# Turning the rows of two expert mixtures: DMA transposes on ScalarE's queue in place of TensorE transposes

## What is computed

```python
# layer 0: x_flat (2048, 256); wg, wu (8, 1024, 256); wd (8, 256, 1024)
hidden = silu(x_flat @ wge.T) * (x_flat @ wue.T)
acc = acc + we[:, None] * (hidden @ wde.T)             # over the 8 experts
# layer 1: W1 (8, 256, 2 * 512), W2 (8, 512, 256), at most 640 rows for an expert
h = einsum('ecd,edf->ecf', exp_batches, W1)
inp, gate = split(h, 2, axis=-1)
exp_out = einsum('eci,eid->ecd', gelu(inp) * gate, W2) # then added up by token with its gates
```

## Time and profile before

| | us |
|---|---|
| median of three runs | 885.04 |
| lowest and highest of them | 881.98, 886.37 |
| span of the profiled execution | 889.0 |
| first mixture's block loop in the profile, about | 289 to 607 |
| second mixture's block loop in the profile, about | 709 to 889 |
| TensorE busy in the span | 700.3 (79%) |
| VectorE busy in the span | 547.8 (62%) |
| ScalarE busy in the span | 403.1 (45%) |
| GpSimd busy in the span | 302.8 (34%) |

### The profile page before, as it was taken

One profiled execution on the slowest core, in us unless ns is written; L12 is line 12 of the kernel. 1 busy time (PEld: TensorE's weight loads), 2 busy tenths in 40 slices (PEclk: granted clock), 3 DMA queues, 4 the chain that ended last, 5 costly groups with the idle time before them and its releaser, 6 DMA issues.

```text
span 889.0 us, 19049 instructions
## 1 busy us (share of the span) xinstructions
PE 700.3 (79%) x6278; PEld 550.1 (62%) x6278; DVE 547.8 (62%) x1322; ACT 403.1 (45%) x720; POOL 302.8 (34%) x306
## 2 busy tenths in 40 slices
PE   5476796989564799999999899996862098898981
PEld 4232454555354688888897798895531087777771
DVE  7768576887836545647556656547696446566441
ACT  1135466576513434646545555442552044546331
POOL 7505301416337422222121131232167414334342
PEclk9689799989776799999999999997875599999996
DMA  4562300601524542536344643425022555464332
GB/s 140 118 141 51 59 2 24 180 24 49 153 81 151 185 129 36 165 51 171 78 126 98 170 112 101 107 39 179 25 101 95 174 170 131 115 147 114 63 55 40
DMA packets 68418, 92.24 MB, mean 104 GB/s; under 512 B 14442, under 2 KB 54435, under 8 KB 68348
## 3 DMA queue, kind: packets, MB, share of 16 engines
q1 hardware_dynamic: 41788, 63.37, 24.1%
q0 software_dynamic: 14592, 16.24, 10.6%
q10 hardware_dynamic: 11968, 11.72, 5.3%
HBM read 64.21 MB, written 29.87 MB: 106 GB/s over the span
## 4 chain that ended last, share of the span: by engine, by line
PE 48%; DVE 18%; issue 11%; ACT 9%; POOL 5%; DMA 5%; ACTq 2%; another core or an unknown queue 1%; DVEq 0%; POOLq 0%; SPq 0%
PE ps L685 45%; POOL rows L631 3%; DVE probs L1726 3%; DVE mx L1591 2%; DMA out_x<-keys,row_to 2%; DVE keys L1804 2%; DMA probs<-rows 2%; ACT probs L1189 1%; ACT probs L1271 1%; ACT expo L1186 1%; DVE keys L1783 1%; ACT probs L1267 1%; PE ps L933 1%; DVE stats L1383 1%; ACTq L1252 1%
## 5 line engine op out<-in xcount | busy, mean ns | idle before, releaser
L1804 DVE TENSOR_TENSOR keys<-probs,ps 128x512 f32<-128x512 f32 x122 | 82.8, 687 | 177.3 <-ACT probs L1267 86.3
L685 PE MATMUL ps<-keys,slot 128*128 128x256 f16 (+1 forms) x1440 | 146.5, 263 | 5.4 <-DVE keys L1783 2.7
L685 PE MATMUL ps<-keys,probs 128*128 128x256 f16 (+1 forms) x1488 | 139.5, 255 | 5.1 <-DVE probs L1405 3.7
L685 PEld LDWEIGHTS ps<-keys,slot 128*128 128x128 f16 x1440 | 127.8, 99 | 22.8 <-issue 5.4
L685 PEld LDWEIGHTS ps<-keys,probs 128*128 128x128 f16 x1488 | 124.2, 98 | 19.0 <-issue 7.2
L575 POOL DMA_INDIRECT attended<-keys,row_to x42 | 67.2, 1601 | 166.0 <-ACT keys L1280 142.2
L1267 ACT ACTIVATE probs<-ps 128x512 f32<-128x512 f32 x122 | 71.4, 598 | 65.9 <-PE ps L685 63.7
L1280 ACT ACTIVATE keys<-ps,carried 128x256 f32<-128x256 f32 x80 | 33.5, 470 | 117.9 <-POOLq L580 41.6
L1809 DVE TENSOR_TENSOR probs<-keys,probs 128x512 f16<-128x512 f32 x122 | 83.3, 688 | 3.6 <-ACT probs L1271 1.9
L1271 ACT CAST probs<-keys 128x512 f16<-128x512 f32 x122 | 74.8, 614 | 22.0 <-DVE keys L1804 21.9
L1726 DVE TENSOR_TENSOR probs<-expo,probs 128x512 f16<-128x512 f32 x80 | 61.1, 775 | 34.1 <-ACT probs L1189 28.2
(11 more groups left out here) (285 smaller groups left out, 1145.7 us busy)
## 6 DMA issues: line engine op xcount, KB each, us to landing
inbox<-in_W SPq DMA_DIRECT2D x24, 512.0 KB, 3.9
probs<-rows ACTq DMA_DIRECT2D x44, 260.0 KB
inbox<-in_wg SPq DMA_DIRECT2D x16, 512.0 KB, 5.2
inbox<-in_wu SPq DMA_DIRECT2D x16, 512.0 KB, 3.7
inbox<-in_wd SPq DMA_DIRECT2D x16, 512.0 KB, 4.2
rows<-zeros SPq DMA_DIRECT2D x16, 260.0 KB
x<-in_x SPq DMA_DIRECT2D x4, 512.0 KB, 6.1
q_out<-queries SPq DMA_DIRECT2D x8, 256.0 KB, 2.1
```

The costliest lines, as they stand in the source:

```text
L685: return pe.matmul(o, l, r, start=start, stop=stop, **kw)
L1804: dve.tensor_tensor(h32[:, j % 2, :], s_act[:, j % 2, :], ps[:, 2 * (j % 2) + 1, :], ALU.mult).then_inc(S(r + "_h32"), 1)
```

## The change

TensorE's 8 transposes for each block go away, and so does VectorE's copy out of PSUM. In their place ScalarE issues two DMA transposes for each block, from `x_raw` to a new buffer `turned_raw` in SBUF, each of 128 rows by 512 float16 values, and VectorE copies `turned_raw` to `xbT`. Rows are loaded and turned one block further ahead: in block g ScalarE turns block g+2 (after its last cast and after `xbT` of block g+1 has been copied) and, behind the scaling of `yb`, loads block g+3. The load waits until the turned rows of block g+2 have landed and their gates have been read, since there is still one `x_raw`. VectorE reads the gates for block g+2 instead of g+1. Ahead of the loop ScalarE loads and turns blocks 0 and 1 and loads block 2. Below, the pieces stand in the order TensorE, ScalarE, VectorE.

```diff
-AHEAD = MAXBLK + 2
+AHEAD = MAXBLK + 3
...
+        turned_raw = sb("turned_raw", [P, 2 * KC, BLK], F16)
...
-                def turn_block(g):
-                    pe.wait_ge(S(r + "_xraw"), g * 16 + 16)
-                    for hf in range(2):
-                        for part in range(4):
-                            last = pe.transpose(psh[:, 6, part * BLK + hf * P:part * BLK + (hf + 1) * P],
-                                                x_raw[:, hf, part * P:(part + 1) * P], identh[:, :])
-                    last.then_inc(S(r + "_xbT_ps"), 1)
...
-                    turn_block(g + 1)
                     pe.wait_ge(S(r + "_y"), g + 1)
...
+                def turn(g):
+                    wait_counted(act, S(r + "_xraw"), g * 16 + 16)
+                    for hf in range(2):
+                        act.dma_start_transpose(turned_raw[:, :, hf * P:(hf + 1) * P], x_raw[:, hf, 0:2 * D]).then_inc(S(r + "_turned"), 16)
+
+                def load_behind(g):
+                    wait_counted(act, S(r + "_turned"), g * 32)
+                    wait_counted(act, S(r + "_carried"), g)
+                    load(g)
...
-                    act.wait_ge(S(r + "_xbT_ps"), g + 3)
-                    act.wait_ge(S(r + "_carried"), g + 2)
-                    load(g + 2)
+                    wait_counted(act, S(r + "_xbT"), g + 2)
+                    turn(g + 2)
                     split(pairs)
                     act.wait_ge(S(r + "_down"), g + 2)
                     wait_counted(act, S(r + "_added"), g + 1)
...
                     ins.then_inc(S(r + "_y"), 1)
+                    load_behind(g + 3)
...
                 load(0)
+                turn(0)
                 act.wait_ge(S(r + "_padded"), 16 * (E - 1))
-                act.wait_ge(S(r + "_xbT_ps"), 2)
-                act.wait_ge(S(r + "_carried"), 1)
-                load(1)
+                load_behind(1)
+                act.wait_ge(S(r + "_xbT"), 1)
+                turn(1)
+                load_behind(2)
...
                 def turned(g):
-                    dve.wait_ge(S(r + "_xbT_ps"), g + 2)
-                    dve.tensor_copy(xbT[:, :, :, :].rearrange("p a b c -> p (a b c)"), psh[:, 6, :]).then_inc(S(r + "_xbT"), 1)
+                    wait_counted(dve, S(r + "_turned"), g * 32 + 32)
+                    dve.tensor_copy(xbT[:, :, :, :].rearrange("p a b c -> p (a b c)"),
+                                    turned_raw[:, :, :].rearrange("p a c -> p (a c)")).then_inc(S(r + "_xbT"), 1)
+
+                def shares(g):
                     own = carried[:, bass.ds(g, 1), :, :].rearrange("p b h d -> p (b h) d")
+                    wait_counted(dve, S(r + "_xraw"), g * 16 + 16)
...
                     turned(g + 1)
+                    shares(g + 2)
...
+                shares(0)
                 turned(0)
+                shares(1)
```

More of the change, by code:

```diff
@@ L970, in one_block @@
                     last.then_inc(S(r + "_down"), 1)
-                pe.sem_inc(S(r + "_xbT_ps"), 1)
                 pe.sem_inc(S(r + "_down"), 1)
@@ L977, in experts @@
                 full_ends = [pe.value_load(tb[0:1, TB_FULL + e:TB_FULL + e + 1], min_val=0, max_val=MAXBLK - 1) for e in range(E)]
-                turn_block(0)
                 for e in range(E):
@@ L1311, in experts @@
                 total = act.value_load(tb[0:1, 8:9], min_val=1, max_val=MAXBLK)
-                wait_counted(act, S(r + "_xraw"), total * 16 + 32)
+                wait_counted(act, S(r + "_xraw"), total * 16 + 48)
+                wait_counted(act, S(r + "_turned"), total * 32 + 64)
             experts(L[0])
```

## The result

The changed kernel takes 1061.53 us (median of four runs, 1059.72 to 1065.57) against 884.08 us of the kernel before on the same chip: 1.20 times the time, 95% interval 1.1975 to 1.2036. The forecast of 945 us had the direction; the loss is three times the 60 us that it summed, and 1061 lies above its range, which ended at 1050.

What follows compares the result with a forecast made beforehand. It took TensorE to bound the first mixture and a chain of waits the second; +35 (second mixture), +6 (first) and +19 us (starts) made +60, put on the median as 945 us, range 885 to 1050.

Steps and rivals of the forecast that it cites:

- What is removed: TensorE's transposes, 0.45 us in each of 15 full first-mixture blocks, 6.7 us; short blocks and second mixture 0.
- VectorE's copy: Copy to xbT, now reading SBUF instead of PSUM, taken at the same 0.68 us.
- The issues: ScalarE's issue of each DMA transpose, taken at 0.39 us; much longer was named a sign of being wrong.
- T: Time from the first transpose's issue to the second's landing, taken as 3.9 us, with ends 2.8 and 6.3.
- Second mixture: New wait loop through ScalarE: periods of 9.94 us, 11.3 in splitting blocks, instead of 8.37; +35 us.
- First mixture: Removal -6.7 us, late silus behind short blocks +10, stalls into short blocks +2.3: together +6 us.
- the cover: First mixture's full blocks: TensorE's two free pairs, 5.24 us, just hide a silu 3.4 us after the start.
- Starts: Both mixtures' starts: turns and loads one behind another make the first silu 9.7 us later; +19 us together.
- Slow turning: Rival: two transposes land one after the other, T 11.9 us, about 1285 us in all; chance 0.12.
- The clock falls: Rival: idle time in the second mixture's short blocks lowers TensorE's clock, 10 us more, 955 us; chance 0.12.
- Short enough to hide: Rival: T below about 1.5 us, no silu late, 18 us of TensorE gained, 876 us; chance 0.07.
- even: Rival: T between 1.5 and 2.1 us, starts' loss against the first mixture's gain, about 887 us; chance 0.06.

Runs made afterwards that it cites:

- e3: Kernel before, plus two DMA transposes per block of a zeroed buffer that nobody reads, issued from ScalarE behind the load of rows: 985.13 us.
- e11: Kernel before with one TensorE transpose per block instead of eight, nothing in their place: 880.09 us against 884.93.
- e1: Changed kernel with transposes reading a zeroed second buffer, so the load of rows doesn't wait for their landing: 961.91 us.
- e2: Changed kernel with SyncE fetching only 128 of 1024 columns of each weight piece for experts 2 to 7: 1006.81 us.
- e8: Changed kernel with loads of rows and DMA transposes issued from SyncE's queue instead of ScalarE's: 916.87 us, 1.0366 of the kernel before.
- e4: Changed kernel with the load of rows, which awaits the landing, moved into the next block behind its first cast: 972.81 us.
- e9: As e8, but in the block loops ScalarE's queue fetches the coming expert's weights: 928.89 us, 1.0492 of the kernel before.
- e6: Changed kernel with every weight fetch cut into 8 DMAs of 128 columns, in runs of 512 B: 1047.23 us.

## Why the prediction was wrong in size

**What bounds the kernel.** Right: waits set the second mixture's pace. Of its 19 scalings before the change 11 wait for GpSimd's addition and 8 for ScalarE's own sequence, but the former have little to spare: e3 gives ScalarE 2.56 us more at a block's end and the mean period grows by 2.4.

**What is removed: 6.7 us.** Right within 2 us: 7 of the 8 transposes gave 4.8 (e11). The gain of 0 in short blocks was 0.35 us each. Full blocks run at 15.72 us from 349.19 to 364.91, as forecast (15.7).

**VectorE's copy, taken at the old 0.68 us.** It takes 0.42 (the changed kernel, in order of time):

```profile
346.13 0.42 DVE L1786 COPY keys<-turned_raw 128x1024 f16<-128x1024 f16 x1
```

From SBUF it is 1.6 times as fast as from PSUM. The 4 times that the Trainium skill ("VectorE: DVE Perf Modes", Rules for kernel authors) gives a 16-bit copy from SBUF to SBUF, read in the forecast as against PSUM, would have saved 0.5 us; 0.26 us were saved. They are the smallest of the errors.

**The issues, taken at 0.39 us each.** Wrong: 1.28 us, three times a load's. The forecast named it as the thing that would make it wrong. In the loop by which it summed, the second issue partly overlaps the landing, so the sum of T came out all the same; but ScalarE is held for 2.56 us and not 0.8 ahead of the scaling, and that was in no term. This is the second step that failed: without any await 78 us of loss remain (e1), and the issues, with nothing awaited and nothing used, cost the kernel before 101 (e3).

**T = 3.9 us, for every block.** This is the first step that failed. In quiet blocks T is 3.8 us, and there the second mixture's loop was right to 2%: periods of 9.75 us where it said 9.94. But in eleven of the thirteen splitting blocks of the two mixtures T is 7 to 10 us, above the forecast's upper end of 6.3. The row that could have told it was in the forecast's hands: the load that took 5.91 us, where the last one took 2.8. Three weight fetches were issued between 805.73 and 809.72, around that load at 808.10, none near the last. The spread was read as uncertainty about T instead of as two kinds of blocks, and nothing was worked out for a transpose beside a fetch of 512 KB. e2 puts 55 us on that.

**Second mixture, +35 forecast, +65 measured.** The nine periods away from splitting blocks have a mean of 10.3 us (9.94 forecast). The five splitting blocks, forecast at 11.3, take 12.3 to 17.8, and the four blocks right behind them 10.0 to 14.3: the scaling that ends a period stands ahead of the wait for the landing, so that this wait falls into the period behind.

**First mixture, +6 forecast, +83 measured: the term most mis-sized.** It had the cover right in quiet full blocks: the silu at 352.47, 3.28 us after the block's start at 349.19, where the forecast said 3.4. By kind of block its 20 periods are, in us:

| periods of the first mixture | before | changed | e2 | e1 | e8 |
|---|---|---|---|---|---|
| six short blocks | 62.0 | 85.0 | 86.7 | 74.2 | 51.2 |
| five behind a short block, four of them splitting | 84.1 | 105.8 | 104.3 | 95.4 | 88.0 |
| six behind a splitting block | 85.2 | 122.9 | 89.9 | 85.3 | 80.8 |
| the other three | 56.7 | 57.4 | 57.2 | 56.6 | 57.7 |

The blocks behind splitting blocks lose 38 us. The forecast left splitting blocks of this mixture out altogether, though seven of 21 are such; with light fetches (e2) 33 of the 38 go, so this is the slow landing. Around short blocks 45 us are lost where the forecast had 12, and light fetches don't help there: in the first of them TensorE stalls 1.94 us inside (0.4 forecast), and its scaling stands behind the issues, so the period is 14.18 us where it was 10.35. Half of these 45 us go without the await (e1); with the issues and the loads off ScalarE too, 4 us remain behind short blocks and the short blocks themselves are faster than before (e8).

**Starts, +19 forecast, +28 measured** (to the first scaling; to the first silu, as the forecast counted, +25). The first silu came at 310.05, forecast 310.2. That is partly luck: the load was issued 3.4 us earlier than before, and the first turning took 9.3 us, since three weight fetches of 512 KB were issued on SyncE's queue between 288.05 and 289.4, behind the clearing of padding. The next turning took 3.8.

**The rivals.** *Slow turning* (T = 11.9 in all blocks) comes near to what happened in eleven splitting blocks, where T was 7 to 10. In quiet ones it fell, and with it the Trainium skill's 1309 ns for a 128x128 by DMA ("VectorE: DVE Perf Modes", The three transpose paths): eight such tiles took 3.8 us, not 10.5. Its 390 ns for TensorE isn't borne out by e11 either, where 7 transposes less for each block gave 4.8 us in all. *The clock falls*: right in kind, 10 us forecast for the second mixture, some 20 us in the first alone (e1). *Short enough to hide* and *even* fell with T.

**The cause.** Shown: the loss is that ScalarE's program issues and awaits the transposes. Without the await it is 100 us less (e1), with a later await 89 us less (e4), with neither on ScalarE 145 us less (e8, which takes the loads of rows off ScalarE too), and the issues, with nothing awaited and nothing used, cost the kernel before 101 us (e3). Of the 33 us that e8 still loses, the second mixture has 23, nearly all in four periods that wait for weights or for GpSimd's addition. That the waits for weights come from turning, rows and fetches in one queue is shown in part (e9); why the addition landed late is open, and so is the rest. What a second `x_raw` would give wasn't tried, and neither were the loads alone on SyncE's queue with TensorE turning, which would tell how much of the 145 us is theirs.

## What to carry to other kernels

A transfer that takes the place of an engine's work is not off that engine's hands if another busy engine must issue it and stand behind its landing: before moving work to a queue, list what stands behind the issue and behind the wait in that engine's program, block kind by block kind. Price a transfer in the blocks where other large transfers run, not by the mean of all. And measure first what the removal can give with nothing in its place: here 4.8 us, against 145 us that hung on which engine issued and awaited the transfers.

## What the runs showed of the hardware

- The issue of a DMA transpose from SBUF to SBUF holds the issuing engine 1.24 to 1.30 us (medians), on ScalarE's and on SyncE's queue, for 128x512 and for 128x256 float16 alike; a load of 260 KB holds it 0.40 us.
- A transpose of 128x512 lands 2.5 us after its issue begins when the DMA engines are otherwise quiet, 5.8 to 8.7 us beside weight fetches of 512 KB, and 3.2 to 4.9 us (second mixture) when these are cut into runs of 512 bytes (e6), for which ScalarE then waits longer.
- TensorE's clock stood at 0.50 in the 3 us that were read behind an idle time of 5.36 us; the same 48 matmuls took 7.65 us in place of 5.40.
